# A four-layer graph network on one core: 391 edge and 391 source scatters divided anew among the stages

## The chip, the core and the metric

The kernel runs on one core of a Trainium2 chip. The core has TensorE (PE, matrix products), VectorE (DVE), ScalarE (ACT), GpSimd (POOL) and SyncE (SP); the last three issue DMAs here, and sixteen DMA engines carry them all. The metric is the device time of one execution in microseconds, as the median of several runs. A shorter time is better.

## What is computed

The reference is a chain of eight blocks on a node table x of 3125 x 256 and 50000 edges, each block adding to x. Cut to what matters here:

```python
x = x + L0_gnn(layernorm(x), edges)          # out[dst] += h[src] * norm
x = x + L0_ffn(layernorm(x))                 # shared expert + 2 of 8 private experts, 256 -> 1024 -> 256
x = x + L1_gnn(layernorm(x), edges, edge_attr)
#   msg = relu(x[src] + edge_attr); agg = zeros.at[dst].add(msg)
#   h = relu(batchnorm((x + agg) @ W1 + b1)) @ W2 + b2; norms; residual
x = x + L1_ffn(layernorm(x))                 # 1 of 32 experts, 256 -> 64 -> 256
x = x + L2_gnn(layernorm(x), edges)          # softmax over the edges of one source node
x = x + L2_ffn(layernorm(x))                 # 2 of 16 experts
x = x + L3_gnn(layernorm(x), edges)          # 4-head attention over the edges of one target node
x = x + L3_ffn(layernorm(x))
```

## The kernel before

Nodes are worked on in T = 25 tiles of 125 rows, edges in 415 tiles of 128. The edges have to be known in two orders: by target node (for L0, L1 and L3) and by source node (for L2). The ranks are computed at the start. Two sets of indirect DMAs on POOL's queue then carry the data to its sorted place, a column of 128 edges each, EC = 391 columns in either set:

- **Edge scatters** (`EdgeRows`, L879): 128 rows of 256 floats of `edge_attr`, 128 KB, from an SBUF buffer to rows of the table `eaS`. SP first loads the column into the buffer (L891). There are NB = 5 buffers, named idxS, locS, wiS, eaB and eidD in the profile, used in turn: POOL's scatter waits for the load, and SP's load of column c waits until the scatter of column c - 5 has landed. `eaS` is read in L1's sum over edges, so SP waits for the last edge scatters at the end of L0's experts (`landed`, in `table_sync`).
- **Source scatters** (`SourceScatter`, L803): 128 integers from `pkS` to the table `recs`. They need no load; at most four are under way. SP waits for the last of them in `L2Project` and then reads `recs` back (L2201), from which VectorE computes the indices of L2 (L2242).

All these scatters are side work: each stage that has room issues some per tile, as written in the `gpsimd` function of the stage, and the classes keep count of how many are done, so that a later stage goes on where the last one stopped. SP's loads are counted the same way in the `sync` functions. Between two stages all five queues meet (`meet`): none goes on before the last has arrived.

The stages that matter, in order, with what they issue before the change:

- sort, and L0's sum over edges: 45 + 22 edge scatters.
- L0's router together with the shared expert (`fused_*`): per tile 3 edge scatters once the tile's hidden half is computed, then 3 or 4 once the output of the tile before is; 162 in all. SP loads 7 or 6 columns per tile, with four 2 MB loads of private weights in the same queue (L1358).
- L0's private experts (`expert_*`), 56 tiles of 128 tokens. POOL gathers the tile's rows (L1522) and then, from tile 2 on, issues 3 edge and 2 source scatters; TensorE flips the gathered rows (L1584, L1585) and multiplies (L1598, L1609). ACT issues 1 MB of weights per tile.
- L1's sum over edges: none.
- L1's MLP (`L1Mlp`): in the first dense layer one source scatter at every second tile, 12; in the second layer 6 for each of 7 pieces, 42; on the way back one per tile, 25.
- The second router (`scores_*`): 2 source scatters per tile, 50; then 19 while tokens are grouped, and 1 per expert tile from tile 2 on, 54.
- L2's projections (`L2Project`): 3 source scatters per tile, gated by TensorE's product of the tile before, and behind the last tile whatever is left, 6.

Of the kernel before, what the change touches and what calls it, by code (L numbers as in the profile page):

```python
# [19 lines left out]
T = 25  # L20
# [196 lines left out]
def load(s, ticket, dst, src):  # L217

    sem, value = ticket
    if value > 16:  # L220
        s.wait_ge(sem, value - 16)
    s.dma_start(dst, src).then_inc(sem, 16)


def row_index(ix, k):
    return bass.IndirectOffsetOnAxis(ap=ix[:, k:k + 1], axis=0)
# [261 lines left out]
class Sort:  # L488
# [217 lines left out]
    def gpsimd(self, g):  # L706
        K = self.K
        g.wait_ge(*self.rows.n(1))
        g.wait_ge(*self.ini_d.n(1))
        for c in range(self.NS):  # L710
            if c >= 4:
                g.wait_ge(*self.sent.n(c - 4))
            if 3 <= c < 64:
                g.wait_ge(*self.deg.n(6 * (c - 2)))
            elif c >= 64:
                g.wait_ge(*self.placed.n((3 * (c - 62)) // 2))
            g.indirect_dma_start(out=K.recd, out_offset=bass.IndirectOffsetOnAxis(ap=self.rowD[:, c:c + 1], axis=0),
                                 in_=self.codeI[:, c:c + 1], in_offset=None).then_inc(*self.sent.up(c))
# [336 lines left out]
class Moe:  # L1055
# [289 lines left out]
    def fused_sync(self, s):  # L1345
        K, a, E = self.K, self.K.a, self.E
        load(s, self.t_rw, self.rw, a[self.router])
        load(s, self.t_rb, self.rb[0:PT, :], a[self.rbias])
        load(s, self.t_b1s, self.b1s, a["L0_b1s"])
        load(s, self.t_wb, K.wb[:, :], a["L0_b2s"])  # L1350
        load(s, self.t_b1, self.b1[0:self.hc, :], a[self.key + "b1"])
        load(s, self.t_b2, self.b2[0:E, :], a[self.key + "b2"])
        for t in range(T):
            s.wait_ge(*self.hid[0].n(t + 1))
            i = t // self.every
            if t % self.every == 1 and i < self.n_w:
                lo, hi = i * self.step, min((i + 1) * self.step, E)
                s.dma_start(self.w2s[:, lo * self.w2:hi * self.w2].rearrange("p (e c) -> p e c", c=self.w2),  # L1358
                            a[self.key + "w"].rearrange("p (e c) -> p e c", c=self.ecols)[:, lo:hi, self.w2off:]).then_inc(*self.weights.up)
            self.side.edges.sync(s, 7 if t % 2 else 6)  # L1360

    def fused_gpsimd(self, g):
        for t in range(T):
            if t:
                g.wait_ge(*self.hid[1].n(t + 1))
            self.side.edges.gpsimd(g, 3)
            if t:
                g.wait_ge(*self.out2.n(t))
            self.side.edges.gpsimd(g, 4 if t % 2 else 3)

    def fused_vector(self, v):
        K, own = self.K, self.K.own_v
# [142 lines left out]
    def expert_gpsimd(self, g):  # L1515
        K = self.K
        for k in range(self.NT):
            if k >= self.RX:
                g.wait_ge(*self.e_flip.n(k - self.RX + 1))
            if self.shared and k >= 4:  # L1520
                g.wait_ge(*self.e_hid[1].n(k - 3))
            g.indirect_dma_start(out=self.xg[k % self.RX], out_offset=None, in_=K.tabA, in_offset=row_index(self.tix, k)).then_inc(*self.rows_in.up(k))  # L1522
            if self.shared and k >= 2:
                self.side.edges.gpsimd(g, 2)
                if k >= 6:
                    g.wait_ge(*self.e_y.n(k - 5))
                self.side.edges.gpsimd(g, 1)
                self.side.source.gpsimd(g, 2)
            elif self.side and k >= 2:
                self.side.gpsimd(g, 1)  # L1530

# [385 lines left out]
class L1Mlp:  # L1917
# [29 lines left out]
        load(s, self.t_vec, self.vec, a["L1_vec"])  # L1947

    def gpsimd(self, g):
        for t in range(0, T - 1, 2):  # L1950
            if t:
                g.wait_ge(*self.biased.n(t))
            self.source.gpsimd(g, 1)
        for i in range(7):
            g.wait_ge(*self.second.n(2 * i + 1))
            self.source.gpsimd(g, 6)
        for t in range(T):
            g.wait_ge(*self.back.n(t + 1))
            self.source.gpsimd(g, 1)

    def flip(self, p, t):
        K, acc = self.K, self.tab.acc
# [1507 lines left out]
def build(nc, a, out):  # L3470
    ctx = ExitStack()
    with ctx:
        K = Kit(nc, ctx, a, out)
        sort = Sort(K)
        edges = EdgeRows(K, sort)
# [3 lines left out]
        source = SourceScatter(K, sort_s)  # L3479
# [2 lines left out]
        l0_out = L0Out(K, sort.acc, sort.t_b)  # L3482
        K.close()
        m0 = Moe(K, 0, 8, 2, 1024, 56, "L0_", "L0_wr", "L0_br", 4096, shared=True, post=post_add,
                 side=SideWork(edges, (0, 3, 0), source, (0, 2, 0)))
        l1 = L1Table(K)
        l1_sum = EdgeSum(K, l1.acc, edge_rows=edges)
        K.close()
        l1_mlp = L1Mlp(K, l1, source)
        K.close()  # L3490
        m1 = Moe(K, 1, 32, 1, 64, 56, "L1f_", "L1f_wr", "L1f_br", 384, post=post_relu,
                 side=SideWork(None, None, source, (2, 1, 19)))
        l2 = L2Project(K, source)
        K.close()
        l2_max = L2Max(K, l2)
# [279 lines left out]
```

## Time and profile before

| | us |
|---|---|
| median of 3 runs | 5876.17 (5872.45 to 5876.91) |
| the profiled execution | 5874.7 |
| its span | 5872.7 |
| POOL busy in the span | 3579.9 (61%) |
| TensorE busy | 4469.9 (76%) |
| VectorE busy | 3651.1 (62%) |

The shares of the whole span say little, since every stage has another limit. The rows below are therefore from single stages. In the rows of a time line the columns are: start in us from the start of the span, duration in us, engine, line, operation, output<-inputs, count; the brackets hold the engine's idle time before the instruction and what ended it. "issue" means that it waited for nothing that the profile shows.

### The profile page before, as it was taken

The page shows a single profiled execution, that of the slowest core. Times are in us where ns is not written, and L with a number is a line of the kernel's source. Part 1 is how long each engine was busy: PE and PEld are TensorE (multiplying, and loading weights), DVE is VectorE, ACT ScalarE, POOL GpSimd, SP SyncE. Part 2 cuts the span into 40 slices and gives each one's busy share as a digit, 9 for nine tenths or more (in the row PEclk, how much of TensorE's full clock was granted, in tenths as well). Part 3 has the DMA queues.
Part 4 walks back from the last instruction along what each step waited for, and adds up shares of the span by engine and source line. Part 5 has one row for each costly group of instructions (what it writes and reads, how often), then busy time and mean ns, then how long its engine had stood idle before and what let it go on. Part 6 is the DMA issues. An engine that isn't in the chain of part 4 may idle for free. (4 is left out here: it accounts for less than half of the span.)

```text
span 5872.7 us, 84688 instructions
## 1 busy us (share of the span) xinstructions
PE 4469.9 (76%) x19486; PEld 2920.1 (50%) x19486; DVE 3651.1 (62%) x12388; ACT 1837.0 (31%) x6462; POOL 3579.9 (61%) x3819
## 2 busy tenths in 40 slices
PE   4668777778867777659488866888597688878868
PEld 3333335767843334434355535666495333346636
DVE  9987643301037775533466677888524688888875
ACT  0000002222323333212423334554143455544421
POOL 3767775676657775575577756776124477756620
PEclk9985667989976567655899988999697799999978
DMA  1053336687757675023254447987374488854400
GB/s 54 25 165 102 104 105 167 218 263 240 248 153 208 206 205 127 25 77 99 68 134 126 127 87 245 286 285 230 122 211 134 131 230 233 231 139 139 144 20 22
DMA packets 526942, 901.08 MB, mean 153 GB/s; under 512 B 101137, under 2 KB 383712, under 8 KB 518016
## 3 DMA queue, kind: packets, MB, share of 16 engines
q0 software_dynamic: 164160, 449.94, 27.7%
q1 hardware_dynamic: 301866, 317.09, 17.4%
q10 hardware_dynamic: 60438, 128.64, 7.1%
q8 instruction: 182, 2.98, 0.2%
q14 instruction: 296, 2.42, 0.1%
HBM read 725.55 MB, written 169.76 MB: 152 GB/s over the span
## 5 line engine op out<-in xcount | busy, mean ns | idle before, releaser
L1021 PE MATMUL bank<-small 128*125 128x256 f32 x1660 | 818.7, 615 | 277.8 <-DVE small L988 173.0
L969 POOL DMA_INDIRECT small<-tabA,idxD x830 | 803.2, 968 | 275.2 <-issue 181.3
L1021 PEld LDWEIGHTS bank<-small 128*125 128x125 f32 x1660 | 373.9, 278 | 721.7 <-DVE small L988 409.8
L1554 DVE COPY small<-bank 128x256 f32<-128x256 f32 x176 | 74.7, 425 | 737.9 <-PE bank L1609 737.9
L803 POOL DMA_INDIRECT recs<-pkS,rowS x391 | 384.8, 984 | 231.3 <-issue 100.4
L2907 POOL DMA_INDIRECT small<-tabC,idxD x415 | 408.5, 984 | 190.7 <-SPq L202 64.6
L2645 POOL DMA_INDIRECT big<-tabB,idxD x415 | 396.2, 955 | 195.6 <-issue 89.6
L2432 POOL DMA_INDIRECT big<-tabT,idxS x415 | 415.8, 1002 | 139.0 <-issue 109.7
L1000 DVE TENSOR_TENSOR big<-big,bank 125x256 f32 x830 | 346.5, 417 | 231.2 <-PE bank L1021 216.2
L2985 PE MATMUL bank<-big,cst 128*125 128x512 f32 x830 | 426.7, 595 | 0.5 <-ACT big L2972 0.5
L1598 PE MATMUL bank<-small,big 128*128 128x128 f32 (+1 forms) x3040 | 413.7, 295 | 0.0
L1609 PE MATMUL bank<-big 128*128 (+1 forms) x1520 | 391.0, 404 | 2.2 <-issue 2.2
L1598 PEld LDWEIGHTS bank<-small,big 128*128 128x128 f32 (+1 forms) x3040 | 382.0, 202 | 19.3 <-issue 19.2
L2971 ACT ACTIVATE big<-cst,small 128x128 f32<-128x128 f32 x830 | 286.9, 393 | 239.7 <-DMA small<-tabC,idxD 237.5
L1522 POOL DMA_INDIRECT small<-tabA,small x176 | 169.0, 960 | 312.4 <-PE bank L1585 162.5
L3045 POOL TENSOR_TENSOR small<-small,big 128x256 f32<-128x256 f32 x415 | 249.1, 631 | 166.2 <-ACT big L3107 151.6
L2295 PE MATMUL bank<-big,small 125*128 x1245 | 212.2, 278 | 138.4 <-DMA big<-tabB,idxD 72.3
L1609 PEld LDWEIGHTS bank<-big 128*128 128x128 f32 (+1 forms) x1520 | 286.8, 199 | 51.4 <-issue 20.8
L1638 ACT ACTIVATE big<-bank,small 128x128 f32<-128x128 f32 (+1 forms) x760 | 220.8, 367 | 256.7 <-PE bank L1598 255.1
L3133 PE MATMUL bank<-small 128*125 128x260 f32 x830 | 289.9, 436 | 1.3 <-ACT small L3097 1.3
L1010 ACT ACTIVATE small<-small 128x256 f32<-128x256 f32 x415 | 172.9, 417 | 375.2 <-DVE small L993 375.2
L2954 DVE TENSOR_REDUCE small<-bank 125x4 f32<-125x512 f32 x415 | 282.3, 680 | 0.0
(484 smaller groups left out, 10370.2 us busy)
## 6 DMA issues: line engine op xcount, KB each, us to landing
small<-eaS SPq DMA_DIRECT2D x830, 128.0 KB
big<-in_L_w ACTq DMA_DIRECT2D x56, 1024.0 KB
eaS<-small SPq DMA_DIRECT2D x415, 128.0 KB, 2.8
big<-in_L2f_w ACTq DMA_DIRECT2D x64, 512.0 KB
ytab<-small ACTq DMA_DIRECT2D x176, 128.0 KB
big<-rowsS SPq DMA_DIRECT2D x52, 256.0 KB
small<-rowsD SPq DMA_DIRECT2D x52, 256.0 KB
big<-rowsD SPq DMA_DIRECT2D x52, 256.0 KB
```

Of the source, the lines that this page charges most:

```text
L803: g.indirect_dma_start(out=K.recs, out_offset=bass.IndirectOffsetOnAxis(ap=K.rowS[:, c:c + 1], axis=0), in_=K.pkS[:, c:c + 1], in_offset=N ...
L969: g.indirect_dma_start(out=self.gb[k % self.RG], out_offset=None, in_=K.tabA, in_offset=row_index(K.idxD, k)).then_inc(*self.got.up(k))
L1000: v.tensor_tensor(rows, rows, K.bank[k % 4][0:PT, 0:D], ALU.add).then_inc(*self.added.up)
L1021: p.matmul(self.K.bank[k % 4][0:PT, 0:D], self.oh[k % self.RO][:, 0:PT], self.gb[k % self.RG], start=True, stop=True).then_inc(*self.summe ...
L1598: m = p.matmul(self.hidden(k, hf)[0:hc, j * 128:j * 128 + 128], w1[:, c * F + f * 128:c * F + f * 128 + hc], xT[:, c, :], start=(c == 0), ...
L1609: m = p.matmul(K.bank[6 + k % 2][:, 0:D], self.hT[k % self.RT][0:hc, f * 128:(f + 1) * 128], K.big[0:hc, bass.ds(where + f * D, D)], start ...
L2432: g.indirect_dma_start(out=self.rows(k)[:, 0, :], out_offset=None, in_=K.tabT, in_offset=row_index(K.idxS, k)).then_inc(*self.got.up(k))
L2645: g.indirect_dma_start(out=self.gb[k % self.RB], out_offset=None, in_=K.tabB, in_offset=row_index(K.idxD, k)).then_inc(*self.got.up(k))
L2907: g.indirect_dma_start(out=self.gb[k % self.RG], out_offset=None, in_=K.tabC, in_offset=row_index(K.idxD, k)).then_inc(*self.got.up(k))
L2971: a.activation(self.diagonals(k, h, 1), K.ident, ACT.Copy, scale=gb[:, D + h:D + h + 1])
L2985: p.matmul(b, K.ones[:, 0:PT], self.dg[k % self.RD], start=False, stop=True).then_inc(*self.field.up)
L3133: p.matmul(K.bank[4 + k % 4][0:PT, 0:AW], self.oh[k % self.RO][:, 0:PT], self.gb[k % self.RG], start=True, stop=True).then_inc(*self.summe ...
```

## The change

Only the numbers that divide the side work are changed; the gathers, the computation and the total of either set of scatters stay.

```diff
@@ fused_sync
-            self.side.edges.sync(s, 7 if t % 2 else 6)
+            self.side.edges.sync(s, 5)
@@ fused_gpsimd
-            self.side.edges.gpsimd(g, 4 if t % 2 else 3)
+            self.side.edges.gpsimd(g, 2)
@@ expert_gpsimd
-                self.side.edges.gpsimd(g, 1)
-                self.side.source.gpsimd(g, 2)
+                self.side.edges.gpsimd(g, 2)
+                self.side.source.gpsimd(g, 1)
@@ L1Mlp.gpsimd
-        for t in range(0, T - 1, 2):
+        for t in range(T - 1):
             if t:
                 g.wait_ge(*self.biased.n(t))
-            self.source.gpsimd(g, 1)
+            self.source.gpsimd(g, 2)
@@
         for t in range(T):
             g.wait_ge(*self.back.n(t + 1))
-            self.source.gpsimd(g, 1)
+            self.source.gpsimd(g, 2)
@@ build
-                 side=SideWork(edges, (0, 3, 0), source, (0, 2, 0)))
+                 side=SideWork(edges, (0, 4, 0), source, (0, 1, 0)))
@@
-                 side=SideWork(None, None, source, (2, 1, 19)))
+                 side=SideWork(None, None, source, (1, 1, 19)))
```

| stage | edge scatters before, after | source scatters before, after |
|---|---|---|
| sort and L0's sum | 67, 67 | |
| L0's router and shared expert | 162, 125 | |
| L0's private experts | 162, 199 | 108, 54 |
| L1's MLP: dense, second layer, way back | | 12 + 42 + 25, 48 + 42 + 50 |
| second router, grouping, experts | | 50 + 19 + 54, 25 + 19 + 54 |
| L2's projections | | 81, 99 |

In the experts the 199 edge scatters run out in tile 51; tiles 52 to 55 issue a gather and one source scatter. TensorE, VectorE and ScalarE have the same instructions in the same order in both kernels.

On POOL, in the private experts, before (L1522 is the gather of a tile, L879 an edge scatter, L803 a source scatter):

```order
L1522 DMA small<-tabA,small 128x256
L879 DMA eaS<-wiS,rowE 56839x256
L879 DMA eaS<-eaB,rowE 56839x256
L879 DMA eaS<-eidD,rowE 56839x256
L803 DMA recs<-pkS,rowS 53639x1 x2
L1522 DMA small<-tabA,small 128x256
```

and at the same place after the change:

```order
L1522 DMA small<-tabA,small 128x256
L879 DMA eaS<-idxS,rowE 56839x256
L879 DMA eaS<-locS,rowE 56839x256
L879 DMA eaS<-wiS,rowE 56839x256
L879 DMA eaS<-eaB,rowE 56839x256
L803 DMA recs<-pkS,rowS 53639x1
L1522 DMA small<-tabA,small 128x256
```

Between two gathers there are five scatters in either; one that needs a loaded buffer has taken the place of one that doesn't.

On POOL, from the last gathers of L0's combination (L1657) over L1's sum (L969) to the experts of L1, as a difference; the middle rows are all of L1's MLP, the second router and the grouping:

```order
 L1657 DMA small<-ytab,small 128x256 x50
 L969 DMA small<-tabA,idxD 128x256 x415
-L803 DMA recs<-pkS,rowS 53639x1 x148
+L803 DMA recs<-pkS,rowS 53639x1 x184
 L1522 DMA small<-tabA,small 128x256 x3
```

The stretch has 36 source scatters more: 61 more in L1's MLP, 25 fewer in the router.

On POOL, from the last gathers of L1's combination over L2's projections to the first gathers of L2 (L2432):

```order
 L1657 DMA small<-ytab,small 128x256 x25
-L803 DMA recs<-pkS,rowS 53639x1 x81
+L803 DMA recs<-pkS,rowS 53639x1 x99
 L2432 DMA big<-tabT,idxS 128x257 x415
 L2549 MEMSET big 125x6400
```

The 18 more stand behind those of the last tile, and SP's read of `recs` waits for all of them.

## Rows read from the trace of the kernel before

**Rows 1.** Table of stretches: length, busy us (count) per engine, granted clock, DMA share, GB/s.

```profile
core 0: us, PE busy (x) PEld busy (x) DVE busy (x) ACT busy (x) POOL busy (x), PEclk, DMA share, GB/s
942.60:1201.30 258.70, 198.75 (x1404) 185.05 (x1404) 75.15 (x350) 67.54 (x229) 155.16 (x161) 0.89 0.64 209
...
1201.30:1680.70 479.40, 427.29 (x2800) 395.83 (x2800) 44.41 (x187) 150.09 (x505) 315.86 (x328) 0.94 0.76 244
...
1147.00:1201.30 54.30, 0.00 (x0) 0.00 (x0) 0.37 (x1) 0.00 (x0) 35.81 (x38) 0.54 0.65 212
...
1300.00:1400.00 100.00, 89.38 (x593) 82.30 (x592) 13.15 (x60) 30.82 (x104) 66.03 (x69) 0.95 0.78 247
```

**Rows 2.** Time line of POOL, end of L0's router stage.

```profile
1153.29 0.96 POOL L879 DMA_INDIRECT eaS<-idxS,rowE  x1 [6.39 <-DMA idxS<-in_ea]
...
1202.26 0.96 POOL L879 DMA_INDIRECT eaS<-eaB,rowE  x1 [0.30 <-issue]
```

**Rows 3.** Time line of VectorE at the ends of four stages.

```profile
1202.60 0.59 DVE L1546 COPY small<-small 128x8 f32 x3 [55.23 <-issue]
...
2474.91 0.18 DVE L245 BATCH_NORM_AGGREGATE mv<-st 125x2 f32<-125x6 f32 x1
...
2540.96 0.18 DVE L1281 CAST small<-small 125x25 f32<-125x25 uint32 x1 [20.81 <-SPq L202]
...
2923.32 0.38 DVE L2242 TENSOR_SCALAR idxS<-big 128x416 int32<-128x416 int32 x1 [18.74 <-DMA big<-recs]
```

**Rows 4.** Time line of TensorE in L0's private experts: first instruction of a tile.

```profile
1210.71 0.45 PE L1584 MATMUL bank<-cst,small 128*128 128x128 f32 x1 [64.33 <-DMA small<-tabA,small]
...
1406.69 0.33 PE L1584 MATMUL bank<-cst,small 128*128 128x128 f32 x1 [3.26 <-DMA small<-tabA,small]
...
1415.62 0.27 PE L1584 MATMUL bank<-cst,small 128*128 128x128 f32 x1
...
1422.87 0.27 PE L1584 MATMUL bank<-cst,small 128*128 128x128 f32 x1
...
1656.96 0.32 PE L1584 MATMUL bank<-cst,small 128*128 128x128 f32 x1
```

**Rows 5.** Time line of POOL in L0's private experts.

```profile
1417.28 0.97 POOL L879 DMA_INDIRECT eaS<-eidD,rowE  x1 [0.30 <-issue]
1418.56 0.96 POOL L879 DMA_INDIRECT eaS<-idxS,rowE  x1 [0.30 <-issue]
...
1429.39 0.96 POOL L879 DMA_INDIRECT eaS<-eidD,rowE  x1 [2.26 <-DMA eidD<-in_ea]
...
1444.68 0.96 POOL L879 DMA_INDIRECT eaS<-eidD,rowE  x1 [1.65 <-DMA eidD<-in_ea]
```

**Rows 6.** Line 891, 1203 to 1650: who waited for its loads (us, times).

```profile
  POOL eaS L879: 52.2, 31
```

**Rows 7.** Time line of POOL in L1's MLP.

```profile
2319.57 0.96 POOL L803 DMA_INDIRECT recs<-pkS,rowS  x1 [3.01 <-ACT big L2021]
2323.57 0.96 POOL L803 DMA_INDIRECT recs<-pkS,rowS  x1 [3.05 <-ACT big L2021]
...
2375.18 0.96 POOL L803 DMA_INDIRECT recs<-pkS,rowS  x1 [18.62 <-PE bank L1998]
...
2428.73 0.96 POOL L803 DMA_INDIRECT recs<-pkS,rowS  x1 [0.82 <-PE bank L2009]
...
2471.76 1.14 POOL L803 DMA_INDIRECT recs<-pkS,rowS  x1 [0.75 <-PE bank L2009]
```

**Rows 8.** Time line of SP's DMA queue, end of L2's projections.

```profile
2920.00 0.35 SPq L2201 DMA_DIRECT2D big<-recs  x1
```

**Rows 9.** Line 879, 1203 to 1650: from issue to landing.

```profile
DMA to landing us min/median/max: 2.6/5.1/9.3
```

**Rows 10.** Time line of SP's DMA queue in L0's private experts.

```profile
1420.84 0.33 SPq L891 DMA_DIRECT2D eidD<-in_ea  x1
...
1435.80 0.33 SPq L891 DMA_DIRECT2D eidD<-in_ea  x1
```

**Rows 11.** POOL's instructions by line, 2807 to 2916.

```profile
L803 POOL DMA_INDIRECT recs<-pkS,rowS x78 | 78.3, 1004 | 38.0 <-issue 20.5 <-DMA recs<-pkS,rowS 9.1 <-PE bank L934 8.4
```

## The prediction

> **What bounds the kernel now.** I read the table of stages first, because the kernel is a row of stages with a meeting of all five queues between them, and a change can only act where the queue that arrives last at a meeting is touched. Then I read, at the end of each touched stage, which engine worked last, and inside the stage what that engine waited for.
>
> Five stages are touched. Router with shared expert (942.6 to 1201.3): TensorE and VectorE are done by 1147.4, and POOL alone goes on; 39 edge scatters stand back to back from 1153.29 to 1202.26, one every 1.27 us, and VectorE idles 55.23 us before its next work, TensorE 64.33 us [rows 1 to 4]. POOL is the bound. The private experts (1201.3 to 1680.7): TensorE needs 7.25 us for a fed tile (1415.62 to 1422.87), while POOL issues six indirect DMAs per tile, 1.27 us from start to start, so 7.6 us without any wait; the row with 3.26 us of idle ahead of L1584 shows TensorE waiting for the gathered rows [rows 4, 5]. POOL bounds here too, and adds 52.2 us in 31 waits for edge rows to load [rows 6]. The first and the last tile stand at 1210.71 and 1656.96: 8.11 us per tile over 55 [rows 4]. L1's MLP (2302.4 to 2475.1): VectorE's last work ends at 2475.1, POOL's last scatter starts at 2471.76, so VectorE bounds with POOL close behind [rows 3, 7]. The second router (2475.1 to 2540.9): VectorE idles 20.81 us while POOL finishes its 50 scatters [rows 3]. L2's projections (2795.6 to 2928.3): SP reads the table of records at 2920.00, behind POOL's scatters, and VectorE idles 18.74 us for that read [rows 3, 8]. POOL is the bound.
>
> **The change, part by part.** Nothing is added to or taken from the 391 edge and 391 source scatters; they move between stages. What counts is what a scatter costs where it leaves and where it arrives.
>
> *Router stage, 162 edge scatters become 125.* The 37 that go come off the back-to-back stretch behind TensorE's end: 37 x 1.267 = 46.9 us. POOL would then arrive near 1201.3 - 47 = 1154, still behind VectorE's 1147.4, so the gain isn't cut short. The fourth load of weights, which now stalls POOL for 6.39 us at 1153.29 [rows 2], is issued with tile 19 and so falls inside the 125. Bounds: -54 us if POOL keeps up fully with TensorE (VectorE's end then decides), -35 us if the gates of each tile, which POOL now passes late and hence for free, cost it half a microsecond per tile. I take -47, the count of rows.
>
> *Expert tiles, 3 edge + 2 source scatters become 4 + 1.* The number of POOL slots per tile stays six, so at first sight this is free. It is not a swap of like for like, because an edge scatter needs one of five SBUF buffers, and a buffer is free for the next scatter only after its scatter has landed, SP's next load has been issued and landed. Between two uses of one buffer lie five edge scatters: 5/3 of a tile now, 12.7 us at 7.6 us per tile; 5/4 of a tile afterwards, 9.5 us. Against that stands the chain. A scatter lands after a median of 5.1 us, between 2.6 and 9.3 [rows 9]. The load moves the same 128 KB over the same sixteen engines, and I give it the same 5.1 us. Two chains are whole in the rows: eidD is scattered at 1417.28, loaded at 1420.84 and scattered again at 1429.39 after a wait; that scatter is followed by the load at 1435.80 and the next scatter at 1444.68, again after a wait [rows 5, 10]. These take 12.1 and 15.3 us; they are the long ones, since POOL waited for them. With 0.3 us of POOL's own gap the usual chain is 10.5 us. So the slack per turn goes from +2.2 to -1.0 us. With 199 edge scatters in the stage, 40 turns short by 1.0 us are 40 us; the waits that come from scatter in the latencies, 52.2 us over 162 scatters now, grow with the count to 64. That is 104 against 52, **+52 us**. The least, if only the mean chain binds: a tile takes 4/5 of 10.5 = 8.4 us, 0.29 more than now, over 50 tiles +14. I take +50, near the upper, because latencies don't become even when the ring is tight. Queued behind each waiting scatter on POOL is the next tile's gather, and TensorE waits for that [rows 4], so a wait passes through one to one. The 17 slots saved over the stage give nothing: they lie in the last four tiles, and TensorE's tiles are 7.25 us there already.
>
> *L1's dense part, 12 source scatters become 48.* POOL starts one every two tiles, 4.00 us apart with 3.05 us idle (2319.57, 2323.57), and stands idle 18.62 us before the second layer [rows 7]. Two per tile need 2.53 us where a tile takes 2.0: POOL falls behind by 0.53 us a tile and ends at about 2313.6 + 46 x 1.265 = 2371.8 (2319.57 is the gate of tile 4, so that of tile 1 is three tiles before), and the next part begins at 2375.18. Cost 0; the idle time covers it with 3 us to spare, and nobody reads the table yet.
>
> *L1's way back, 25 become 50.* Now POOL follows VectorE's tiles, 1.89 us apart, its scatters lasting up to 1.14 us beside VectorE's work [rows 7]. Fifty from 2428.73 on take 1.14 + 0.30 = 1.44 us each until 2475.1 (32 of them) and 1.26 after: the last starts at about 2496.5, 21 us behind VectorE's end; at 1.26 throughout 2490.7, 16 us. I take +19.
>
> *Second router, 50 become 25.* At 65.8 us for 50, 25 take 33 us, less than the 45 us that VectorE needs: it last worked at 2540.96 - 20.81 = 2520.15 [rows 3]. The stage shrinks by the idle time of VectorE, 20.8 us; I take -21. With the part before: -2.
>
> *L2's projections, 81 become 99.* The six left over become 24 behind the last tile. POOL is last already and runs without a break, so each of the 18 more is paid in full: 18 x 1.265 = 22.8; at the mean of the stretch, 78 in 78.3 + 38.0 - 8.4 = 107.9 us, it is 25 [rows 11]. I take +23. SP's read waits for all of them and VectorE for SP's read [rows 3, 8].
>
> **Sum.** -47 + 50 + 0 + 19 - 21 + 23 = +24 us. The profiled execution took 5874.7 us with a span of 5872.7; it lies 1.5 us under the median of the runs, 5876.17, which is within their spread. 5874.7 + 24 = 5898.7, so **5899 us**, slower by 0.4%. A measurement of this kernel can tell about 0.2% (12 us) from no change.
>
> **Rivals.** *The ring doesn't bind* (faster). If the chain of scatter and load stays under 9.5 us with its spread covered, the expert stage keeps its 479 us and the sum is -26: 5849 us. It decides at a chain of 9.5 us against the 10.5 that I use. For it: in the router stage POOL runs back to back, five scatters in 6.3 us, from 1153 to 1202 with no wait for a load [rows 2], so the chain can be under 6.3 us. Against it: the DMA engines are busy 0.65 of the time there and 0.78 between 1300 and 1500, beside 1 MB of weights per tile [rows 1], and the two chains shown took 12 and 15 us. The Trainium skill (DMA: Bandwidth & Descriptors, Anatomy of one DMA — SWDGE path) speaks for this rival: it gives a DMA about 2.0 us plus its bytes at 436 GB/s, by which 128 KB would take 2.3 us and the chain under 5 us, as an estimate. The median landing of 5.1 us in this stage says that rule doesn't hold beside the weights.
>
> *The ring relieves itself* (no change). Slower tiles space the 1 MB weight loads out, which shortens every chain. If it comes to 9.5 us on average, only the spread grows, 12 to 25 us instead of 50: 5861 to 5874 us.
>
> *Contention feeds on itself* (much slower). One edge more per tile adds 256 KB of traffic, where the rest is about 2 MB. If loads take 6.7 us rather than 5.1, as the waited ones in the rows do and more, a chain is 12.1: 40 x 2.6 + 64 - 52 = +116 and 5965 us.
>
> **How the numbers follow.** Forecast 0.60, from 5882 (experts +33) to 5915 (+66); the ring doesn't bind 0.18; relieves itself 0.14; feeds on itself 0.08. The range runs from 5848, so that the first rival is in, to 5925, leaving out the last. Faster: 0.18 and a part of the third case, 0.22. Same: 0.15. Slower: 0.63.
>
> **What would show it.** The router stage 45 to 50 us shorter, with TensorE's gap ahead of the first expert tile down from 64 us to under 20. In the expert stage POOL's waits for loads at about 100 us instead of 52 and 9 us or more per tile; if they stay near 52 the first rival holds. POOL last at L1's MLP by some 20 us and no longer at the second router; SP's read of the records 23 us later against the stage's start. I'd be wrong if the landing of a scatter beside the weights falls well under 5 us, or if POOL in the router stage ends later than 1160 because it passes the tile gates late.

## The result and the profile after

The changed kernel takes 5892.36 us (median of 9 runs, 5883.26 to 5906.85) where the kernel before takes 5872.45 us on the same chip (9 runs, 5861.85 to 5887.75). The ratio is 1.004 with a 95% interval of 1.0027 to 1.0053: slower by 16 to 31 us. The prediction was 5899 us, slower by 0.4%, with a range from 5848 to 5925.

The profiled execution of the changed kernel took 5886.8 us with a span of 5885.0 us, 12.3 us more than the span before. All stages that the change doesn't touch agree within 2 us each. The touched ones, in the table of stretches of the changed kernel (columns as in [rows 1]; L0's router, L0's experts, L1's MLP, second router, L2's projections):

```profile
943.30:1154.80 211.50, 199.29 (x1404) 185.65 (x1404) 75.17 (x350) 67.65 (x229) 119.58 (x124) 0.97 0.65 211
1154.80:1675.30 520.50, 440.60 (x2800) 409.19 (x2800) 44.49 (x187) 150.09 (x505) 299.52 (x311) 0.92 0.76 243
2296.20:2483.70 187.50, 118.80 (x616) 86.66 (x616) 92.00 (x288) 60.19 (x158) 131.24 (x137) 0.75 0.04 7
2483.70:2528.30 44.60, 31.15 (x150) 29.84 (x150) 18.68 (x103) 9.80 (x26) 26.85 (x29) 0.50 0.51 169
2782.90:2936.80 153.90, 61.99 (x250) 42.14 (x250) 58.72 (x189) 69.38 (x226) 99.13 (x99) 0.80 0.21 59
```

Each length is the time from one meeting of all queues to the next, so the lengths add up to the span. Set beside the kernel before (all five from its meetings in the same way; the second is 479.46, which [rows 1] with its rounded bounds gives as 479.40):

| stage | before | after | difference | forecast |
|---|---|---|---|---|
| L0's router | 258.7 | 211.5 | -47.2 | -47 |
| L0's experts | 479.5 | 520.5 | +41.0 | +50 |
| L1's MLP | 172.8 | 187.5 | +14.7 | 0 + 19 |
| second router | 65.8 | 44.6 | -21.2 | -21 |
| L2's projections | 132.7 | 153.9 | +21.2 | +23 |
| sum | | | +8.5 | +24 |

The remaining 3.8 us of the span's 12.3 are spread over stages with the same instructions, in both directions.

**End of the router stage.** Time lines of POOL, TensorE and VectorE of the changed kernel, against [rows 2, 3, 4]:

```profile
1154.40 0.96 POOL L879 DMA_INDIRECT eaS<-idxS,rowE  x1 [0.54 <-issue]
1155.66 0.96 POOL L879 DMA_INDIRECT eaS<-locS,rowE  x1 [0.30 <-issue]
1156.93 0.98 POOL L1522 DMA_INDIRECT small<-tabA,small  x1 [0.30 <-issue]
...
1164.18 0.45 PE L1584 MATMUL bank<-cst,small 128*128 128x128 f32 x1 [16.66 <-DMA small<-tabA,small]
...
1156.08 0.53 DVE L1546 COPY small<-small 128x8 f32 x3 [7.57 <-issue]
```

POOL still arrives last, but now 6 us behind VectorE instead of 54. VectorE's idle time is 7.57 us instead of 55.23, TensorE's 16.66 instead of 64.33: both gave back 47.7 us.

**The experts.** Who waited for line 891's loads, and how long they took from issue to landing, 1156 to 1650 (before: [rows 6]). Such a landing row covers only the buffers whose landing records are complete in the trace, here one of the five:

```profile
  POOL eaS L879: 99.3, 52
...
DMA to landing us min/median/max: 2.0/3.9/9.0
```

What ended POOL's idle time ahead of the edge scatters (the 199 of the stage and the router's last), same stretch (us, times):

```profile
  issue: 45.1, 146
  DMA eidD<-in_ea: 26.5, 11
  DMA eaB<-in_ea: 23.1, 13
```

Two things are to be seen. The waits went from 52.2 to 99.3 us. And 146 of the scatters waited for nothing but POOL's ordinary 0.31 us: the time is in a quarter of the scatters, 1.9 us each.

Last tiles of the stage, time line of TensorE:

```profile
1637.07 0.27 PE L1584 MATMUL bank<-cst,small 128*128 128x128 f32 x1
1644.32 0.27 PE L1584 MATMUL bank<-cst,small 128*128 128x128 f32 x1
1651.56 0.27 PE L1584 MATMUL bank<-cst,small 128*128 128x128 f32 x1
```

From 1164.18 to 1651.56 it is 8.86 us per tile on average against 8.11 before [rows 4]. The fed tile is unchanged, 7.25 us.

**The source scatters.** Time lines of POOL and VectorE in L1's MLP and the second router, against [rows 3, 7]:

```profile
2364.22 0.96 POOL L803 DMA_INDIRECT recs<-pkS,rowS  x1 [0.31 <-issue]
2369.95 0.96 POOL L803 DMA_INDIRECT recs<-pkS,rowS  x1 [4.78 <-PE bank L1998]
...
2482.77 0.96 POOL L803 DMA_INDIRECT recs<-pkS,rowS  x1 [0.30 <-issue]
...
2469.73 0.18 DVE L245 BATCH_NORM_AGGREGATE mv<-st 125x2 f32<-125x6 f32 x1
...
2528.54 0.96 POOL L803 DMA_INDIRECT recs<-pkS,rowS  x1 [4.77 <-SPq L202]
```

The dense part's 48 scatters end at 2364.22 and POOL then idles 4.78 us, so they cost nothing. On the way back POOL's last scatter starts 13 us behind VectorE's last instruction. In the second router it is POOL that waits 4.77 us at the meeting.

End of L2's projections: SP's read of the records and VectorE's first use in the time line, and then POOL's instructions by line between 2795 and 2922 (before: [rows 3, 8, 11]):

```profile
2928.63 0.35 SPq L2201 DMA_DIRECT2D big<-recs  x1
...
2931.57 0.38 DVE L2242 TENSOR_SCALAR idxS<-big 128x416 int32<-128x416 int32 x1 [39.34 <-DMA big<-recs]
```

```profile
L803 POOL DMA_INDIRECT recs<-pkS,rowS x95 | 95.2, 1002 | 40.3 <-issue 26.9 <-PE bank L934 8.2 <-DMA recs<-pkS,rowS 5.3
```

SP's read stands 145.7 us behind the stage's start, against 124.4 before, and VectorE waits 39.34 us instead of 18.74.

### The profile page after: what moved, and what is told of

It reads as the page before. It is cut to its first block and busy times, and to the rows that moved or that the text cites. A ratio compares the mean times of both kernels' runs of the same rounds, so it can differ in the third digit from the quotient of the medians.

```text
span 5885.0 us, 84700 instructions
## 1 busy us (share of the span) xinstructions
PE 4509.0 (77%) x19486; PEld 2945.1 (50%) x19486; DVE 3651.3 (62%) x12388; ACT 1835.7 (31%) x6462; POOL 3578.4 (61%) x3819
## 5 line engine op out<-in xcount | busy, mean ns | idle before, releaser
L969 POOL DMA_INDIRECT small<-tabA,idxD x830 | 804.2, 969 | 276.1 <-issue 191.6
L2432 POOL DMA_INDIRECT big<-tabT,idxS x415 | 414.8, 1000 | 139.7 <-issue 109.1
L803 POOL DMA_INDIRECT recs<-pkS,rowS x391 | 380.7, 974 | 176.0 <-issue 108.8
L1598 PE MATMUL bank<-small,big 128*128 128x128 f32 (+1 forms) x3040 | 426.5, 301 | 0.0
L1598 PEld LDWEIGHTS bank<-small,big 128*128 128x128 f32 (+1 forms) x3040 | 395.5, 208 | 19.1 <-issue 19.0
L1522 POOL DMA_INDIRECT small<-tabA,small x176 | 169.0, 960 | 322.5 <-PE bank L1585 164.2
L1609 PEld LDWEIGHTS bank<-big 128*128 128x128 f32 (+1 forms) x1520 | 287.4, 200 | 51.2 <-issue 21.2
```

The lines of the kernel that those rows point to most:

```text
L803: g.indirect_dma_start(out=K.recs, out_offset=bass.IndirectOffsetOnAxis(ap=K.rowS[:, c:c + 1], axis=0), in_=K.pkS[:, c:c + 1], in_offset=N ...
L969: g.indirect_dma_start(out=self.gb[k % self.RG], out_offset=None, in_=K.tabA, in_offset=row_index(K.idxD, k)).then_inc(*self.got.up(k))
L1598: m = p.matmul(self.hidden(k, hf)[0:hc, j * 128:j * 128 + 128], w1[:, c * F + f * 128:c * F + f * 128 + hc], xT[:, c, :], start=(c == 0), ...
L1609: m = p.matmul(K.bank[6 + k % 2][:, 0:D], self.hT[k % self.RT][0:hc, f * 128:(f + 1) * 128], K.big[0:hc, bass.ds(where + f * D, D)], start ...
L2432: g.indirect_dma_start(out=self.rows(k)[:, 0, :], out_offset=None, in_=K.tabT, in_offset=row_index(K.idxS, k)).then_inc(*self.got.up(k))
```

## The experiments

Two theories on the experts were to be told apart. Mine: the chain from a scatter to the next load of its buffer is too long for five buffers, and POOL's waits for it lengthen the stage one to one. Rival: the stage is longer for the traffic of one more edge column per tile, with any number of buffers. The numbers below on the stage are from single profiled executions; where a ratio is given, there were several runs.

**1. The moves of source scatters undone** (the experts keep 4 + 1):

```diff
@@ L1Mlp.gpsimd
-        for t in range(T - 1):
+        for t in range(0, T - 1, 2):
-            self.source.gpsimd(g, 2)
+            self.source.gpsimd(g, 1)
@@ way back
-            self.source.gpsimd(g, 2)
+            self.source.gpsimd(g, 1)
@@ build, second router
-                 side=SideWork(None, None, source, (1, 1, 19)))
+                 side=SideWork(None, None, source, (2, 1, 19)))
```

> The changed kernel with only the source scatters of L1's MLP (12 + 42 + 25) and of the second router (50) put back as they were; the edge scatters stay as changed, so 60 source scatters are left behind the last tile of L2's projections instead of 24. My theory (each is paid where the last queue is POOL): L1's MLP 172.8 us instead of 187.5, the second router 65.8 instead of 44.6, L2's projections 153.9 + 36 x 1.265 = 199 us, the whole 5885 - 15 + 21 + 45 = 5936 us of span. Rival (the scatters behind the last tile are partly hidden by SP's own stores): L2's projections under 185 us.

Measured 5938.0 us, beside 5863.39 for the kernel before (median of 7 runs on that chip). L1's MLP 173.3, second router 67.0, L2's projections 200.6. The two rows at the end of the projections:

```profile
2989.68 0.35 SPq L2201 DMA_DIRECT2D big<-recs  x1
...
2992.59 0.38 DVE L2242 TENSOR_SCALAR idxS<-big 128x416 int32<-128x416 int32 x1 [86.53 <-DMA big<-recs]
```

What isn't issued earlier stands behind the last tile of the projections, and every scatter there is paid: 36 more took 200.6 - 153.9 = 46.7 us, 1.30 us each. With 54 source scatters driven out of the experts, the other moves are worth 200.6 + 67.0 + 173.3 - 153.9 - 44.6 - 187.5 = 55 us. The experts, which have the same instructions here as in the changed kernel, took 534.7 us, with 108.2 us of waits (48 times) over the whole stage. So a single execution of this stage is uncertain by about 14 us. The span of 5936.0 us met the expected 5936 partly by luck: the experts were 14 us longer than in the changed kernel, and stages that the edit doesn't touch some 18 us shorter.

**2. The router stage alone** (125 edge scatters there, the experts back to 3 + 2, the 37 that are left behind the gathers of L0's combination; source scatters as before). Against the kernel before:

```diff
@@ fused_sync
-            self.side.edges.sync(s, 7 if t % 2 else 6)
+            self.side.edges.sync(s, 5)
@@ fused_gpsimd
-            self.side.edges.gpsimd(g, 4 if t % 2 else 3)
+            self.side.edges.gpsimd(g, 2)
@@ table_sync
+        self.side.edges.sync(s, EC)
```

> The kernel before with only the router stage changed: 5 edge scatters per tile there, experts 3 + 2 as before, source scatters as before; the 37 edge scatters over run behind the gathers of L0's combination. My theory (the cost in the experts comes from four edge scatters per tile on five buffers): router stage 211 us as in the changed kernel, experts 475 to 485 us with some 50 us of POOL waiting for loads, the combination 77 + 30 to 45 us. Rival (the experts are slower because the stage starts right behind the router stage, with DMA queues still full and TensorE never idle): experts 500 us or more with 3 + 2 as well.

Measured 5864.39 us. Router 210.8, experts 468.2 with 37.2 us of waits (26 times), combination 138.0. The first two go my theory's way: the router's 47 us are kept and the experts pay nothing. They are even 7 us under the range of 475 to 485 and 11 us under the kernel before, on the same 3 + 2; this too is within what single executions of the stage differ by. The third was expected at 107 to 122 us and is 61 us longer than the 77.0 of before. Time line of POOL and of SP's queue there:

```profile
1682.99 1.00 POOL L879 DMA_INDIRECT eaS<-eidD,rowE  x1 [0.30 <-issue]
...
1728.97 0.96 POOL L879 DMA_INDIRECT eaS<-idxS,rowE  x1 [0.30 <-issue]
...
1726.23 25.40 SPq L1752 DMA_DIRECT2D tabA<-big  x25
```

The 37 scatters take 47 us, and SP can't store the combined table (L1752) before it has issued the last edge load: another 25.4 us behind them. A side load placed in a queue ahead of main work is paid in that queue too, which my expectation left out.

**3. Four buffers instead of five in the kernel before**, from column 229 on (the first of the experts). `EdgeRows` keeps its columns in parts, each with its own list of buffers; this core of the edit is, with other numbers, that of all the following kernels that have more or fewer than five buffers:

```diff
@@ EdgeRows
-        self.got = K.ring(self.NB, EC, keep=True)
-        self.put = K.ring(self.NB, EC, "gather", keep=True)
+        spare = [K.big[:, 26880 + i * D:26880 + (i + 1) * D] for i in range(7)]
+        self.parts = [(0, 229, self.buf), (229, EC, (self.buf + spare)[:4])]
```

> The kernel before with four instead of five edge buffers from the first expert tile on (column 229), everything else as it was: no DMA more and no byte more per tile. My theory (the turn of the buffers against the chain of scatter and load): a turn is 4/3 of a tile, 10.1 us at 7.6 us a tile, against a chain of 10.5: slack -0.4 us, so POOL waits 80 to 95 us for loads instead of 52 and the experts take 505 to 515 us instead of 479. Rival (what costs is the traffic, one edge row set more per tile): experts stay at 480 us.

Measured 5910.01 us, experts 530.3. The edit adds twelve lines, so that in these kernels the edge scatter stands on L891 and its load on L903. Who waited for the loads from 1203 to 1700 (us, times; over the whole stage it is 95.5 us in 36), and then the table of stretches for the stage:

```profile
  POOL eaS L891: 92.5, 35
```

```profile
1199.60:1729.90 530.30, 443.25 (x2800) 410.33 (x2800) 44.53 (x187) 150.07 (x505) 315.72 (x328) 0.92 0.69 220
```

Here the columns per tile are those of before, 3 + 2, and the traffic per us is lower than before (220 GB/s against 244 [rows 1]). The waits and the stage grow all the same, by more than the 505 to 515 us expected. More traffic isn't needed for the loss; a shorter turn of the buffers is enough.

**4. Ten buffers in the changed kernel**, from column 67 on (`(0, 67, self.buf), (67, EC, (self.buf + spare)[:10])`).

> The changed kernel with ten edge buffers from the router stage on (column 67), the further five in columns of SBUF that are free in these stages: same scatters, same bytes. My theory: a turn is 10/4 of a tile, 19 us, so POOL hardly waits for loads (under 20 us), a tile takes 7.6 to 8.0 us and the experts 440 to 455 us instead of 520; the whole 65 to 80 us less than the changed kernel, about 5815. Rival (contention: one edge column more per tile fills the DMA engines, and TensorE's gathers and weights come late whatever the buffers): experts 505 us or more, with TensorE waiting for gathers or weights while POOL doesn't wait.

Measured 5787.54 us (4 runs), ratio 0.9876 (0.9856 to 0.9896). Experts 440.1. First the stage in the table of stretches:

```profile
1145.00:1585.10 440.10, 414.09 (x2800) 381.34 (x2800) 44.51 (x187) 150.09 (x505) 299.31 (x311) 0.98 0.88 287
```

Who waited for the loads (us, times), and the loads from issue to landing:

```profile
  POOL eaS L891: 6.1, 10
...
DMA to landing us min/median/max: 2.8/7.7/15.1
```

The scatters from issue to landing:

```profile
DMA to landing us min/median/max: 4.4/6.7/8.9
```

Same instructions, same bytes, 80 us less in the stage, and the waits are gone. The single transfer isn't faster: loads land after 7.7 us in the median instead of 3.9, scatters after 6.7. More of them are under way, the DMA engines are busy 0.88 of the time and move 287 GB/s instead of 243. So the traffic was no limit at five buffers; the rival falls. The whole was expected near 5815 us and is 27 us less: the experts are at the low end of their range, the router stage gave another 7 us (204.2 after 211.5), and this chip runs the kernel before in 5863.39 us against 5872.45; the rest isn't accounted for. The landing rows are from two of the ten buffers for the loads and one for the scatters.

**5. Seven buffers in the changed kernel** (`[:7]`).

> The changed kernel with seven buffers instead of five from column 67 on. A buffer's turn is then 7/4 of a tile, 13.3 us at 7.6 us per tile, against a chain of about 10.5 us: my theory expects nearly as little waiting as with ten, 5 to 20 us, and the experts at 440 to 460 us. Rival (waits come from rare long chains of 15 us and more, not from the mean): over 40 us of waits and the experts at 480 or more.

Measured 5832.62 us, beside 5871.96 (7 runs) on that chip; experts 471.2. Who waited (us, times), and then the stage in the table of stretches:

```profile
  POOL eaS L891: 41.0, 37
```

```profile
1150.50:1621.70 471.20, 424.33 (x2800) 392.69 (x2800) 44.04 (x187) 150.56 (x505) 300.66 (x311) 0.96 0.82 268
```

The 41 us of waits miss my 5 to 20 and meet the rival's bound of over 40; the stage, 471.2 us, lies between my 440 to 460 and the rival's 480. A turn of 13.3 us covers the mean chain, which is 11.4 us in this kernel's trace, and yet 37 scatters waited. So the length of single chains counts, not their mean, as the rival had it.

**6. Ten buffers in the kernel before**, on the same chip as 5.

> The kernel before with ten buffers for the edge scatters from column 67 on, nothing else changed. My theory (the wait for a buffer binds in the experts, also in the kernel before): no waits for loads in the experts, that stage 435 to 445 us against 480, the router stage 215 to 225 instead of 259, because the last weights no longer stall the loads and POOL keeps up; the rest as before; in all 5,790 to 5,810. If this holds, the change is worth about nothing with ten buffers, since both kernels then lie within 20 us. Rival (the experts of the kernel before are bound by POOL's six issues per tile, and the wait was small): 5,840 or more.

Measured 5806.69 us (4 runs), ratio 0.989 (0.9872 to 0.9907). Router 225.4, experts 444.4 with 3.4 us of waits:

```profile
1170.00:1614.40 444.40, 412.91 (x2800) 383.94 (x2800) 44.41 (x187) 150.09 (x505) 320.56 (x333) 0.97 0.84 264
```

The router stage is at the upper edge of what was expected, 215 to 225 us, and the rest inside. The kernel before lost 35 us in its experts as well, and 33 in its router. With ten buffers the whole change is worth 0.9876 against 0.9890, whose intervals overlap.

**7. Half of the weights.** In the changed kernel with its five buffers, the first-layer weights that ACT loads per expert tile are halved. From the fourth tile on the second half is what an earlier tile left there, so that this kernel doesn't compute the experts' result:

```diff
@@ expert_weights
-        src = self.K.a[self.key + "w"][:, bass.ds(at.at(k), 2 * self.F)]
-        a.dma_start(self.w1s[k % self.RW], src).then_inc(*self.w_in.up(k))
+        n = self.F if self.layer == 0 and k >= self.RW else 2 * self.F
+        src = self.K.a[self.key + "w"][:, bass.ds(at.at(k), n)]
+        a.dma_start(self.w1s[k % self.RW][:, 0:n], src).then_inc(*self.w_in.up(k))
```

> The changed kernel, but from the fourth expert tile of L0 on only the first half of the tile's first-layer weights is loaded, 512 KB instead of 1 MB (the other half is left over from earlier tiles, so part of the computation is changed); matrix products, scatters, gathers and the five buffers stay. TensorE never waits for these loads in the changed kernel, so that by themselves they cost nothing. My theory (a scatter and its buffer's next load take 4 to 16 us because they share the DMA engines with the weights, and POOL waits for the long ones): the waits for loads fall from 99 to between 10 and 45 us and the expert stage from 520 to between 445 and 480; in all 5,810 to 5,850. Rival (the long chains come from the indirect DMAs and POOL's queue itself): waits stay over 80 us, the stage at 505 or more, in all 5,870 or more.

Measured 5792.5 us, beside 5854.05 for the kernel before; experts 450.3. Who waited from 1156 to 1560 (us, times; over the whole stage it is 22.5 us in 28), and from issue to landing of the loads, of one buffer:

```profile
  POOL eaS L879: 19.8, 27
...
DMA to landing us min/median/max: 2.0/2.5/6.3
```

TensorE never waits for these weights in the changed kernel. Taking half of them away still gives 70 us in the stage. Over the loads of all five buffers, the longest tenth begins at 4.8 us instead of 7.8. So the long chains come from running beside 1 MB of weights per tile. Whether it is the DMA engines or the memory behind them that is shared was not tested. The whole, 5792.5 us, is under the 5810 to 5850 expected, while the stage is inside its range.

**8. The source scatters where POOL waits anyway**, with ten buffers: five per tile in the four last expert tiles and 8 behind, 12 in L0's combination, 9 in L1's sum, 48 + 42 + 38 in L1's MLP, 25 in the second router, 20 in the grouping, 54 + 22 in L1's experts, 5 in the combination, 37 in L2's projections:

```diff
@@ expert_gpsimd
-                self.side.source.gpsimd(g, 1)
+                self.side.source.gpsimd(g, 1 if k < 51 else 2 if k == 51 else 5)
...
+        if self.side:
+            self.side.source.gpsimd(g, 8 if self.shared else 22)
@@ combine_gpsimd
+        if self.side:
+            self.side.source.gpsimd(g, 12 if self.layer == 0 else 5)
@@ L1Mlp.gpsimd, way back
-            self.source.gpsimd(g, 2)
+            self.source.gpsimd(g, 2 if t < 13 else 1)
@@ L2Project.gpsimd
-            self.source.gpsimd(g, 3)
+            self.source.gpsimd(g, 2 if t < 12 else 1)
@@ build, second router
-                 side=SideWork(None, None, source, (1, 1, 19)))
+                 side=SideWork(None, None, source, (1, 1, 20)))
@@ gpsimd, behind L1's sum
+            source.gpsimd(g, 9)
```

> The changed kernel with ten buffers, and the source scatters put where POOL waits anyway: five per tile in the last four expert tiles of L0 and 8 behind, 12 in L0's combination, 9 in L1's sum, 48 + 42 + 38 in L1's MLP, 25 in the second router, 20 in the grouping, 54 + 22 in L1's experts, 5 in the combination, and 37 instead of 99 in L2's projections. Expected: against the changed kernel with ten buffers (5,788 on another chip) 12 us less in L1's MLP and 33 us less in L2's projections, in all 5,740 to 5,755, a ratio of 0.979 to 0.982 to the kernel before. If the table of records isn't what L2's projections wait for, that stage stays at 150 us and the whole at 5,775.

Measured 5758.08 us (4 runs), ratio 0.9805 (0.9789 to 0.9822), the fastest version of all. L1's MLP 173.3, second router 44.9, grouping 37.2, L2's projections 122.5. SP's read and VectorE's use of it:

```profile
2801.10 0.71 SPq L2217 DMA_DIRECT2D big<-recs  x1
...
2809.86 0.38 DVE L2258 TENSOR_SCALAR idxS<-big 128x416 int32<-128x416 int32 x1 [6.53 <-DMA big<-recs]
```

VectorE's wait for the records is 6.53 us of 39.34. The whole is 3 us above the expected 5740 to 5755; the experts took 445.6 us, 5.5 more than in experiment 4.

**9. Three kernels on a slower chip.** These three ran on a chip on which the kernel before takes 6513.78 us (19 runs), and TensorE shows pauses there that no instruction explains, so their times stand apart from all others.

Ten buffers in the kernel before:

> The kernel before, its division of the scatters unchanged, with ten edge buffers from the router stage on. Theory (the buffers' turn sets POOL's waits in both stages): router stage 162 x 1.265 = 205 us plus about 10 us of start and the loads of weights, so 215 to 225 us instead of 258.7; experts 440 us as with 4 + 1 on ten buffers; L1's MLP 172.8, second router 65.8, L2's projections 132; the whole about 5795 us, that is, within 15 us of the changed kernel on ten buffers. Rival (3 + 2 is better than 4 + 1 for another reason than the buffers, for its smaller traffic): experts under 430 us.

Measured 6512.26 us, ratio 1.0001 (0.9985 to 1.0017). Seven buffers in the changed kernel:

> The changed kernel with seven edge buffers from the router stage on: a turn is 7/4 of a tile, 13.3 us, near the 12.7 us of the kernel before. Theory: POOL's waits for loads near those of the kernel before or a little below (25 to 45 us), experts 465 to 485 us. Rival (waits vanish as soon as there is any slack): experts 440 us as with ten.

Measured 6493.36 us. An earlier form of experiment 8, with 32 source scatters in the grouping, 16 behind L1's experts and 31 in L2's projections:

> Ten edge buffers, edge scatters as in the changed kernel, and the source scatters put where POOL arrives early at a meeting: L0's experts 79 (5 a tile in the last four tiles, 8 behind them), L0's combination 12, L1's sum 9, L1's MLP 48 + 42 + 38, second router 25, grouping 32, L1's experts 70, L1's combination 5, so that 31 are left for L2's projections. Theory (a scatter costs nothing while another queue arrives later): experts 440 us, L1's MLP 173 to 175 instead of 188.9, L2's projections 115 to 120 instead of 155.3, the rest as before: 5787.5 - 15 - 38 = 5735 us, 2.2% under the kernel before. Rival (POOL's scatters beside other engines' work slow those, or POOL arrives late at the meetings of the small stages): over 5755 us.

Measured 6496.98 us, ratio 0.9977 (0.9957 to 0.9997). None of the expected times came. In the kernel before with ten buffers, the expert stage there:

```profile
1373.00:1907.60 534.60, 464.94 (x2800) 409.53 (x2800) 44.35 (x187) 147.17 (x505) 314.22 (x326) 0.90 0.66 218
```

It had no wait for a load and still took 534.6 us, 90 more than the same program in experiment 6: TensorE is busy 52 us longer with the same 2800 products. A tile takes 9.2 us there without any wait for a load, which makes a turn of five buffers 15 us, and that would leave little to gain by more of them. The trace points the same way: ahead of the tiles' gathers POOL idles 97.0 us on this chip against 17.0 in experiment 6, and TensorE's products wait 9.0 us for gathered rows against 46.7. So POOL, whose waits the buffers take away, hardly bounds this stage there. Whether this is why the gain is gone stays open, for there is no trace of the unchanged kernel on that chip. The form with 32 in the grouping took 53.6 us for that stage against 39.0 with 19, so experiment 8 puts 20 there.

## Why the prediction was right, point by point

**The router, -47: -47.2.** 37 scatters off a row of 39, which stood at 48.97 / 38 = 1.289 us on average; 37 x 1.289 = 47.7 is just what VectorE and TensorE gave back. The prediction's 1.267 left out seven gaps of 0.37 to 0.49 us in the row. The meeting fell at 1154.8, with 1154 forecast, and POOL's last scatter starts at 1155.66, before the 1160 that would have been a sign of an error. The load of the fourth weights fell inside the 125, as said: POOL waits 5.80 us at 1118.32, while TensorE still works.

**The experts, +50: +41.0.** The waits were forecast at 104 us and are 99.3. A step that was off is the use of that number: each wait contains 0.30 us that POOL has between any two of its DMAs. Taken off, the waits are 99.3 - 52 x 0.3 = 83.7 us after and 52.2 - 31 x 0.3 = 42.9 before, and their difference is 40.8 us, the stage's 41.0. The same account, with the waits of the whole stage, for experiments 1 to 7:

| kernel | experts | waits above 0.30 us | rest |
|---|---|---|---|
| before | 479.5 | 42.9 | 436.6 |
| after | 520.5 | 83.7 | 436.8 |
| source moves undone | 534.7 | 93.8 | 440.9 |
| router alone | 468.2 | 29.4 | 438.8 |
| before, four buffers | 530.3 | 84.7 | 445.6 |
| after, seven | 471.2 | 29.9 | 441.3 |
| after, ten | 440.1 | 3.1 | 437.0 |
| before, ten | 444.4 | 0.1 | 444.3 |
| after, half the weights | 450.3 | 14.1 | 436.2 |

The rest stays within 436 to 446 us while the stage moves by 95: a wait of POOL does pass through one to one, as the prediction had it.

**The chain against the turn: right in size, wrong in its parts.** The prediction took 10.5 us for a chain, put 40 us of the waits down to its mean being above the turn of 9.5, and 12 to its spread. From the trace's issues and landings, matched scatter by scatter (159 in the kernel before, 199 in the changed one), a chain took:

| | turn at 7.6 us per tile | mean | middle half | longest tenth from |
|---|---|---|---|---|
| before | 12.7 | 10.3 | 8.2 to 12.7 | 15.0 |
| before, four buffers | 10.1 | 9.1 | 7.0 to 11.4 | 13.6 |
| before, ten buffers | 25.3 | 11.3 | 9.2 to 13.8 | 14.7 |
| after | 9.5 | 9.3 | 6.6 to 11.5 | 13.4 |
| after, seven buffers | 13.3 | 11.4 | 9.6 to 13.6 | 15.2 |
| after, ten buffers | 19.0 | 14.3 | 12.4 to 15.9 | 16.9 |
| after, half the weights | 9.5 | 7.6 | 6.6 to 8.6 | 9.6 |

Before, 10.5 was close. After, the mean fell to 9.3, under the turn: that is what the rival "the ring relieves itself" said, at 9.5. But its conclusion, 12 to 25 us, didn't follow, because the spread alone made 99 us of waits, in 52 of the scatters and none in 146. A ring of buffers is paid by its long chains: in every row the mean is below the turn, and only in the two with ten buffers, where the turn is also above the start of the longest tenth, are the waits above 0.30 us nearly gone. That the long chains come with the weights' traffic is shown by experiment 7, where the longest tenth begins at 9.6 us and the waits are 22.5. So it is in part luck that this term came near: 40 of its 52 us were reckoned from a mean chain above the turn, which there wasn't.

**The ring doesn't bind: fell**, by 99.3 us of waits where the rival needed about 52. The Trainium skill (DMA: Bandwidth & Descriptors, Anatomy of one DMA — SWDGE (gpsimd) path) would give about 2.3 us for 128 KB, as an estimate; its fit is for DMAs that GpSimd issues, so for the scatters and not for SP's loads. The scatters of the kernel before landed after 2.6 us at the least and 5.1 in the median [rows 9], so this stage doesn't follow it, and no run here shows a scatter with nothing beside it. The loads landed after 2.0 us at the least, 3.9 in the median with five buffers and 7.7 with ten. **Contention feeds on itself: fell.** Loads became shorter, not longer (median 3.7 us in place of 5.3, matched as above), and the same five buffers held the traffic at 243 GB/s, as before (244).

**L1's dense part, 0: shown** by the 4.78 us that POOL idles behind it. **Way back, +19: +14.7.** The scatters stood at (45.0 + 16.0) / 47 = 1.30 us including all waits, and took 0.96 us each; the prediction had given them 1.14 + 0.30 beside VectorE's work. In the kernel before, where each waits for its tile, they did take 1.11 us on average (24 from 2430 to 2475); why they are shorter in a row isn't shown. The prediction's lower figure, 16 us at 1.26 throughout, was the nearer one. The row of the 47 scatters between 2423.4 and 2484:

```profile
L803 POOL DMA_INDIRECT recs<-pkS,rowS x47 | 45.0, 958 | 16.0 <-issue 13.1 <-PE bank L2009 2.7 <-DMA recs<-pkS,rowS 0.3
```

**Second router, -21: -21.2. L2's projections, +23: +21.2.** Both are as the prediction had them; each of the 18 scatters cost 1.18 us.

**The sum.** By the profiled executions the terms give +8.5 us and the span +12.3; by the runs it is 16 to 31, and the forecast was +24. The difference between the two accounts isn't settled. The experts are the likely place: another execution of the same schedule of that stage (experiment 1) took 14 us longer, with 10.1 us more of waits above 0.30 us. So the profiled execution may lie at the short end, and the forecast's +50 for that term can't be called refuted.

**The signs that were named.** TensorE's gap is 16.66 us, under 20. The experts' tiles take 8.86 us, a little under the "9 us or more". POOL is last in L1's MLP by 13 us instead of some 20, and SP's read comes 21.3 us later instead of 23. The scatters still land after a median of 5.0 us (all five buffers, matched as above), so the sign of an error there didn't show; it is the loads that became shorter.

## What to carry to other kernels

Side work that needs a staging buffer isn't worth the same as side work that doesn't, even if each takes one slot of the issuing queue. Compare the turn of the ring (buffers divided by uses per tile, times the tile) with the whole chain of store and refill, and with its longest tenth rather than its mean: at a turn of 13 us and a mean chain of 11.4, POOL still waited 41 us. Before work is moved about among stages that share a ring which waits, try more buffers; here ten of them were worth 1.1% without the moves and 1.2% with them, where the moves alone lost 0.3 to 0.5%. And count for every stage which queue arrives last: the same 1.26 us scatter cost nothing in L1's dense part and its full price behind L2's last tile.

## What the runs showed of the hardware

- A 128 KB transfer's time from issue to landing grew with the number of buffers. With five, seven and ten in the changed kernel the mean chain of scatter and load was 9.3, 11.4 and 14.3 us, while the DMA engines moved 243, 268 and 287 GB/s and were busy 0.76, 0.82 and 0.88 of the time. The longer latency was no loss. A latency measured at one depth isn't the latency at another.
- Loads that nobody waited for had a price: half of the weights' 1 MB per tile left out took the experts from 520.5 to 450.3 us.
- One chip was 11% slower than the others with the same program (6513.78 against 5854 to 5873 us), with TensorE's granted clock at 0.804 instead of 0.834 over the whole span of the kernel before with ten buffers. TensorE's pauses there have no releaser in the trace, and their cause stays open.
